# A new order of TensorE's steps in the attention stage of an attention and feed-forward kernel

## What is computed

```python
x = L0_attn_x                                   # 8192 rows of 512
xn = _layernorm(x)
x = x + infini_attention(xn, W_q, W_k, W_v, W_o, beta) + ffn(xn, ...)

def step(carry, qkv):                           # one segment of 64 rows, 16 heads of 32
    M, z = carry
    q, k, v = qkv
    sq = _sigma(q)                              # elu + 1
    denom_q = jnp.sum(sq * z[:, :, None, :], axis=-1, keepdims=True) + EPS
    A_mem = jnp.matmul(sq, M) / denom_q
    scores = jnp.where(causal, -jnp.inf, q @ k^T / sqrt(dk))
    A_dot = jnp.matmul(jax.nn.softmax(scores, axis=-1), v)
    A_s = beta * A_mem + (1.0 - beta) * A_dot
    sk = _sigma(k)
    denom_k = jnp.sum(sk * z[:, :, None, :], axis=-1, keepdims=True) + EPS
    V_prev = jnp.matmul(sk, M) / denom_k
    M_new = M + jnp.einsum('bhtk,bhtv->bhkv', sk, v - V_prev)
    z_new = z + jnp.sum(sk, axis=-2)
    return ((M_new, z_new), A_s)
# out = A_s of all segments @ W_o.T; 128 segments, one after the other
```

## Time and profile before

| | us |
|---|---|
| median of 3 runs | 1945.66 (1945.05 to 1948.57) |
| the profiled execution's own time | 1945.36 |
| its span, first to last instruction | 1943.6 |
| attention stage, from the span's start to about | 1260 |
| PE busy in the span | 1848.5 (95%) |
| mean granted clock of PE | 0.985 |

### The profile page before, as it was taken

The page is one execution under the profiler, slowest core; times in us unless marked ns, Lnnn a source line. Parts: engine busy times, 40 slices in busy tenths (PEclk is TensorE's granted clock), DMA queues, the critical chain, the costliest instruction groups (busy, mean ns, idle before and its releaser), DMA issues. The chain is left out here.

```text
span 1943.6 us, 72290 instructions
## 1 busy us (share of the span) xinstructions
PE 1848.5 (95%) x32348; PEld 1567.1 (81%) x32348; DVE 1445.2 (74%) x3477; ACT 875.7 (45%) x1494; POOL 148.7 (8%) x179
## 2 busy tenths in 40 slices
PE   6999999999999999999999999879899999879998
PEld 5888888888888888888888888657677777667997
DVE  6888788888887777787777777667588788876222
ACT  4443334343434443444434343325588787764110
POOL 2000000000000000000000000041100000001000
PEclk9999999999999999999999999879999999999999
DMA  4111211121121112111111110236500000015000
GB/s 147 47 46 58 73 52 46 58 74 52 46 74 52 36 36 61 43 36 40 59 41 36 47 51 30 95 95 183 164 26 12 13 12 23 13 41 161 17 12 22
DMA packets 65139, 108.45 MB, mean 56 GB/s; under 512 B 4720, under 2 KB 25216, under 8 KB 64832
## 3 DMA queue, kind: packets, MB, share of 16 engines
q1 hardware_dynamic: 59056, 84.69, 14.0%
q0 software_dynamic: 5776, 19.15, 3.2%
HBM read 59.26 MB, written 27.26 MB: 45 GB/s over the span
## 5 line engine op out<-in xcount | busy, mean ns | idle before, releaser
L1083 PE MATMUL proj<-xnT_high,held 128*128 128x256 f32 x1536 | 235.2, 288 | 3.3 <-DVE xnT_low L782 2.4
L1083 PEld LDWEIGHTS proj<-xnT_high,held 128*128 128x128 f32 x1536 | 203.6, 191 | 9.2 <-DVE xnT_low L782 2.9
L444 POOL TENSOR_TENSOR xs<-xs 128x512 f32<-128x512 f32 x63 | 80.9, 1285 | 1170.0 <-DVE xs L885 1170.0
L1083 PE MATMUL proj<-xnT_low,held 128*128 128x256 f32 x1024 | 163.7, 281 | 0.0
L2088 DVE CUSTOM_DVE_ANT_0 Sm<-Sp,held 128x1023 f32<-128x1023 f32 x128 | 155.5, 1216 | 8.0 <-DVE xs L2076 2.0
L1986 ACT ACTIVATE Sm<-Sm,least 128x1023 f32<-128x1023 f32 x128 | 146.7, 1146 | 14.1 <-DVE least L2088 13.3
L1083 PEld LDWEIGHTS proj<-xnT_low,held 128*128 128x128 f32 x1024 | 140.1, 190 | 0.0
L2141 PE MATMUL Sp<-KS,held 128*128 128x512 f32 x256 | 94.4, 451 | 29.9 <-DVE least L2088 25.6
L506 ACT ACTIVATE Pq<-Pq 128x1024 f32<-128x1024 f32 x63 | 66.9, 1062 | 123.4 <-DVE Pq L848 123.3
L486 ACT ACTIVATE QT<-proj 128x512 f32<-128x512 f32 x64 | 38.1, 595 | 182.4 <-PE proj L1083 182.4
L2038 DVE COPY PTs<-Tp 128x512 f32<-128x512 f32 x128 | 88.3, 690 | 29.7 <-PE Tp L2153 29.2
(11 more groups left out here) (343 smaller groups left out, 4341.2 us busy)
## 6 DMA issues: line engine op xcount, KB each, us to landing
VS<-DV SPq DMA_DIRECT2D x64, 264.0 KB, 3.9
xs<-in_x SPq DMA_DIRECT2D x32, 512.0 KB, 4.8
out_rows<-xs SPq DMA_DIRECT2D x64, 256.0 KB, 2.0
mask_columns<-x1T SPq DMA_DIRECT2D x16, 512.0 KB, 5.2
xs<-in_w SPq DMA_DIRECT2D x16, 512.0 KB, 3.8
xe<-in_x SPq DMA_DIRECT2D x15, 512.0 KB, 3.5
QT<-in_wqT SPq DMA_DIRECT2D x1, 1024.0 KB, 6.5
KT<-in_wkT SPq DMA_DIRECT2D x1, 1024.0 KB, 9.4
```

The lines of the kernel that those rows point to most:

```text
L444: pool.tensor_tensor(Ass[k], T1s[k], T2s[k], ALU.add).then_inc(s_as, 1)
L1083: ins = pe.matmul(bank[:, g * BT:g * BT + BT], w[hw][:, c, o:o + P], xnT[hx][:, c, :], start=n + c == 0, stop=n == 2 and c == G - 1)
```

## The change

PE, head of a half: AST1 goes in front of QT0; A/B 0 goes behind OUT1, directly in front of pv 0; T0 goes behind pv 0. PE, tail: behind memory 1 now come XT0, OUT0, XT1, T3, DEN, mask, scores, (in half 30 mask 1 and scores 1,) dent, SK1. The two banks get new lists. DVE: OUT0's add moves from the head of the next half into the tail of its own, denominators and reciprocals move from the tail into the next half, behind the row maximum and AST1's low part; softmax_part 0 comes ahead of m_next 0, m_next 3 behind the low part of XT1. ACT: AST1's high part ahead of the exponentials, the turned probabilities ahead of the negated A, XT1 ahead of DEN, SK1 last. `last` gets the denominators of the half before and loses OUT0's add. No instruction of work is added or removed.

```diff
--- before.py
+++ after.py
@@ -246,8 +246,8 @@
 
 
 
-        ORDER = (["AST1", "OUT1", "KT0", "KT1", "V1", "SK1", "DEN", "OUT0"],
-                 ["QT0", "QT1", "AST0", "V0", "SK0", "XT0", "XT1"])
+        ORDER = (["AST1", "OUT1", "KT0", "AST0", "V0", "SK0", "OUT0", "DEN"],
+                 ["QT0", "QT1", "KT1", "V1", "XT0", "XT1", "SK1"])
         FIRST = (["XF1", "QT1", "KT1", "V1", "SK1", "DEN"],
                  ["XF0", "QT0", "KT0", "V0", "SK0", "XT0", "XT1"])
 
@@ -534,13 +534,13 @@
             def half(m, p, first=False, ln=True):
                 pn = 1 - p
                 stage1 = True
-                prob(m, 0)
                 if not first:
                     a_t(m, 1)
+                prob(m, 0)
                 if stage1:
                     feature(m, 0, "QT", QT, pn, SCALE, (s_sk, m * 2 + 1))
+                p_turned(m, 0)
                 neg_a(m, 0)
-                p_turned(m, 0)
                 if stage1:
                     feature(m, 1, "QT", QT, pn, SCALE, (s_sk, m * 2 + 2))
                     feature(m, 0, "KT", KT, pn, 1.0, (s_sq, m * 2 + 3))
@@ -555,13 +555,12 @@
                     v_tile(m, pn, 1)
                 if stage1:
                     sk_tile(m, pn, 0)
-                    sk_tile(m, pn, 1)
                 if ln:
                     xT(m, "XT", 0)
+                    xT(m, "XT", 1)
                 if stage1:
                     den_rows(m)
-                if ln:
-                    xT(m, "XT", 1)
+                    sk_tile(m, pn, 1)
 
             high_w(0)
             xT(None, "XF", 0)
@@ -898,11 +897,12 @@
 
             def last(m, p):
                 pn = 1 - p
+                denominators(m - 1, m * 2, p)
+                reciprocals(p)
                 previous_values(m - 1, p)
                 row_max(m, 0, True)
                 less_max(m, 0)
                 m_next(m, 0)
-                out_rows(m - 1, m * 2 - 2, pn, 0)
                 row_max(m, 1, True)
                 less_max(m, 1, 1)
                 low_a(m, m * 2 - 1, 1)
@@ -930,10 +930,10 @@
                 row_max(m, 0)
                 less_max(m, 0)
                 if not first:
-                    out_rows(m - 1, m * 2 - 2, pn, 0)
+                    low_a(m, m * 2 - 1, 1)
+                    denominators(m - 1, m * 2, p)
+                    reciprocals(p)
                 previous_values(None if m == 0 else m - 1, p)
-                if not first:
-                    low_a(m, m * 2 - 1, 1)
                 if stage1:
                     sigma(m, "QT", 0, SQT[:, pn, 0:2, :], s_sq)
                 if look:
@@ -942,8 +942,8 @@
                     offer(m - CHOICE)
                 if not first:
                     out_rows(m, m * 2 - 1, pn, 1)
+                softmax_part(m, 0)
                 m_next(m, 0)
-                softmax_part(m, 0)
                 if first:
                     router(p, wcol[:, 0:2])
                 if m + 1 < AHEAD:
@@ -982,14 +982,12 @@
                 memory_part(m, p, 1)
                 if ln:
                     low_x(m, (m + 2) * 2, "XT", 0)
-                m_next(m, 3)
                 if look:
                     ahead_router(m, 1)
-                if stage1:
-                    denominators(m, n2, pn)
-                    reciprocals(pn)
+                out_rows(m, m * 2, p, 0)
                 if ln:
                     low_x(m, (m + 2) * 2, "XT", 1)
+                m_next(m, 3)
 
             def beta_factors():
                 dve.wait_ge(s_const, 1)
@@ -1277,16 +1275,16 @@
                 n = m + 1
                 n2 = (m + 1) * 2
 
+                if not first:
+                    as_transposes(m, m * 2 - 1, 1)
                 if stage1:
                     feature(m, "QT", wq, 0, ("XT", None if m == 0 else m - 1))
-                if not first:
-                    as_transposes(m, m * 2 - 1, 1)
-                a_and_b(m, p, 0)
                 p_transposes(m, 0)
                 if not first:
                     out_proj(m, 1)
+                a_and_b(m, p, 0)
+                pv(m, mh, p, 0)
                 t_times_m(m, 0)
-                pv(m, mh, p, 0)
                 if stage1:
                     feature(m, "QT", wq, 1)
                 memory(m, p, 0)
@@ -1309,22 +1307,21 @@
                 if stage1:
                     sk_rows(m, n2, 0)
                 memory(m, p, 1)
-                if stage1:
-                    sk_rows(m, n2, 1)
                 if ln:
                     x_transposes(m, m + 2, p, "XT", 0)
+                out_proj(m, 0)
+                if ln:
+                    x_transposes(m, m + 2, p, "XT", 1)
                 t_times_m(m, 3)
                 if stage1:
                     denominators(m, n, pn)
                     mask(m + 1, 0)
                     scores(pn, 0)
-                    den_transposes(m)
                     if m == NB - 2:
                         mask(m + 1, 1, True)
                         scores(pn, 1)
-                if ln:
-                    x_transposes(m, m + 2, p, "XT", 1)
-                out_proj(m, 0)
+                    den_transposes(m)
+                    sk_rows(m, n2, 1)
 
             pe.wait_ge(s_const, 1)
             x_transposes(None, 0, 0, "XF", 0)
```

## The result

The changed kernel took 1980.46 us in the median of 4 runs (1974.97 to 1984.92), the kernel before 1947.12 beside it; the ratio is 1.0167 (95% interval 1.0133 to 1.0201). Run once more later on, it gave 1981.28 us in the median of 5, ratio 1.0160 (1.0142 to 1.0179). So it is slower by 32 us. The direction was forecast, and the time lies 0.5 us inside the range of 1950 to 1981, 14 us above the forecast of 1966.0; the later median lies 0.3 us outside it, beside a kernel before that was slower too (1950.62). The profiled execution of after took 1974.97 us, its span is 1973.2, 29.6 more than before's.

A forecast was written before the change was run, and what follows sets the result against it. PE was taken to bound the attention stage, busy 1232 of 1260 us. Regular halves +15.6, instruction stops +4 and ends +1 made +20.6 on the span of 1943.6; forecast 1966.0 us, range 1950 to 1981.

The forecast's parts named there:

- The new wait at QT0: Head of each half: QT0 waits for SK1's bank copy, 1.43 us from start to start, a wait of 0.51.
- Head and tail: PE's steps per half: head 13.60 us, 2.38 less; tail 2.74 more plus 0.16 wait; together +0.52 a half.
- values and T0 step: Head of a half: values of tile 0 then T0 take 1.38 us together (1.33 to 1.45), saving a switch.
- DEN's wait in the look halves: Tail, first 15 halves, with router rows: DEN waits for OUT0's add, 0.16 us (0 to 0.3).
- Stops for instructions: PE stops at instruction-transfer edges: new ones in 9 of 30 halves, +10 us, old ones -5.7; net +4 (-6 to +12).
- None in the scores: The profile after would show "issue" stops in or behind T0 and no longer in the scores.
- Rival (c): Dense run starves PE: more or longer stops, slow clock behind some; +36 us, 1982; chance 0.13.
- The ends: Last two turns: OUT0 no longer separates denominators from A/B, weight copies come behind SK1's; about +1 us once (-1 to +3).
- (a): Rival: bank free in time for QT0, SK1's copy hidden behind AST1; 1935.2 us; chance 0.08.
- (b): Rival: small new wait and free DEN, +5.4 us, cancel against 5.7 of old stops that go; 1945 us; chance 0.10.
- (d): Rival: PE's clock falls in each half behind the new 0.5 us waits, 43 us more, 2008; chance 0.04.

The follow-up runs named there:

- experiment 4: The changed kernel with SK1 issued in front of the transposes of the denominators (dent) instead of behind them; 1972.75 us, ratio 1.0149.
- experiment 5: The changed kernel with OUT0's add ahead of the second router row on the vector engine in the 15 look halves; 1971.93 us, ratio 1.0150.
- experiment 1: The changed kernel with 120 additional semaphore increments at the start of PE's program; 1973.77 us, ratio 1.0154.
- experiment 9: The kernel before with one repeated 64x33 value product in 16 halves, 14 repeats in half 26 and 38 semaphore increments at the start; 1953.62 us, ratio 1.0027.
- experiment 2: The changed kernel with 168 additional semaphore increments at the start of PE's program; 1997.36 us, ratio 1.0273.

## Why the prediction was right in direction and short in size

**The new wait at QT0: right.** SK1 to QT0 was put at 1.43 (1.30 to 1.55) from rows 4, and measured at 1.38 in every regular half; experiment 4 shows that it is the bank's turn. 0.46 a half over 30 halves makes 13.8 of the 15.3 us forecast. That one turn in the trace of before was worth more than any reasoning on the copy's length.

**Head and tail: right to 0.02 us in the later halves.** Head 13.60 forecast and 13.60 measured (13.49 in halves with a QT0 of 2.80), tail 6.86 forecast and 6.85 measured. In the values and T0 step I took 1.38 of 1.33 to 1.45; it is 1.45. This and the 0.05 at QT0 cancel.

**DEN's wait in the look halves: wrong, 0.16 (0 to 0.3) forecast, 0.52 measured (0.10 in the later halves).** The step put the router row ahead of OUT0's add at "about 0.7 us". Alone it takes 0.69; beside POOL's add it took 1.46. It need not have been a surprise: in the trace of before the same row, at 348.55, takes 1.12, with POOL's add from 347.85 to 349.12:

```profile
347.85 1.27 POOL L444 TENSOR_TENSOR xs<-xs 128x512 f32<-128x512 f32 x1 [17.23 <-DVE xs L885]
...
348.55 1.12 DVE L648 CUSTOM_DVE_ANT_0 ln<-xe,xs 128x512 f32<-128x512 f32 x1
```

In both traces the row ends 0.55 us behind POOL's add, and so, to 0.01, in all 15 look halves of each: 0.69 of its own work begun 0.14 before POOL's end. In experiment 5, where it meets no add, it takes 0.68. By that sum OUT0's add could have been placed. The Trainium skill (SBUF — State Buffer, "🔬 SBUF: two separate sides") has the rule: a vector instruction with two SBUF inputs and a GpSimd instruction that reads SBUF lock the same port pair, and the later one is blocked for the whole of the other. The row reads two SBUF tensors, and the traces agree but for the 0.14. The term was worth 14 x 0.42 = 5.9 us. With the later halves at 0.46 in place of 0.52, the regular halves together came to 14 x 0.86 + 16 x 0.46 = 19.4 us against the 15.6 forecast.

**Stops for instructions: place and kind right, sum short.** Forecast: in or behind T0, 1.3 us each, in 9 of 30 halves, none left in the scores. Measured in the first trace: 7 halves, 0.6 to 1.65 us each, 9.4 in all, 1.5 for a slow clock behind one, and about 2 in small stops at A/B, SK1 and AST1 that I did not have; less the 5.7 that go, +7 against +4 (the spans of halves 1 to 29 leave 6.2 beside the regular halves). The range of -6 to +12 holds it. The +4 itself was summed too low: 9 halves at 1.3 us are 11.7 and not 10. "None in the scores" holds for the first trace; the second has one of 1.5 us there in half 30, and experiment 1 one of 1.2. Rival (c) had 9 stops of 2.2 us and a slow clock of 1.4 us behind 4 of them; in T0 and QT1 there was one such slow clock in each of the two traces. The time came out near this rival's 1982, but by DEN's wait and the ends as much as by stops.

**The ends: +1 (-1 to +3) forecast, +2.9 measured, and half 30 +1.2** (start -0.6, half 0 +0.7, the last turn and all behind it +2.8; half 30 is +1.7, of which 0.46 is the regular half). Half 30 has its own DEN behind OUT0, where T3 to DEN is 0.95, and a KT1 of 3.38. In half 0 the trace of before has a stretch at 1.2 GHz of 6.8 us, the first trace of after none, and the second has one again. The +2.8 is made of two larger terms that I had not seen. The last turn and the start of the feed-forward part are 4.4 us shorter than before's; some 2.9 of it will be before's stop of 1.1 us and slow clock, as experiment 9, which keeps before's order and has no such stop, is 2.9 us ahead at the same place. And one stretch of the feed-forward part, from the 2000th to the 800th product before the end, is 7.2 us longer, though no instruction of it was changed. In order before, after, and experiment 5:

```profile
1662.88:1809.71 146.83, 128.22 (x1208) 103.94 (x1201) 102.64 (x184) 79.02 (x130) 7.88 (x8) 0.99 0.23 73
1685.26:1839.33 154.07, 133.38 (x1209) 108.92 (x1202) 102.74 (x184) 79.12 (x130) 7.66 (x8) 0.94 0.22 69
1686.89:1833.74 146.85, 128.19 (x1208) 103.93 (x1201) 102.68 (x184) 78.88 (x130) 7.89 (x8) 0.99 0.23 73
```

The granted clock is 0.94 in the long one and 0.99 in the short ones, and the second trace of after shows the same (154.2 us at 0.94). Places of edges can't be the cause: all three kernels have the same count of instructions, and experiment 5 takes the 146.85 of before. This stretch alone is more than the 5.6 us by which the span of experiment 5 lies below after's. What makes the clock fall there in one kernel and not in the other stays open. That the time still lies in the range, by 0.5 us, is in part luck: 7.2 us more and 4.4 less, neither of them in the sum, half cancel.

**The rivals.** (a) and (b) needed a free or cheap bank and are out. (d), a clock that falls in each half behind the waits of 0.5 us, did not come: the granted clock of the regular halves is 1.00, with a wait in each. What the Trainium skill tells of another kernel (TensorE: Matmul & The Clock Gate, "A second HAM failure mode: psum-queue depth-cycling") finds no support in the stage here. In halves 1 to 30 of the two traces the clock fell only behind stops of 1.2 us and more, and not behind all of them; half 0 and the part behind the stage have slow stretches of their own.

**What made the median 5.5 us worse than the profiled run** can't be read from a trace of that group, as the slower executions have none. The trace of the later one points the same way: it has the same waits for banks (9.9 and 8.1 us) and the stage 6.7 longer by stops and slow clock. A forecast by one profiled execution can't have that, and my 0.30 us between the profiled run and the median was taken over from a kernel with few stops. Taken together, for the 29.6 us of the profiled execution: about 14 are QT0's turn and 6 DEN's wait in look halves (19.4 with the small terms that go the other way), 6 the stops of halves 1 to 29 with their clock, 1.2 half 30, and 2.9 the ends, in which -4.4 and +7.2 stand against each other. The first two are shown by experiments 4 and 5, the places of the stops by 1 and 2, and the +7.2 has no cause shown.

## What to carry to other kernels

When a move brings short steps together on two banks, look in the trace for a turn of the same kind (product, copy, next product: 1.38 to 1.43 us here) and count what work lies inside it; in-turn work is free, and an order that looks equal in sum is not. When a step comes behind another on the vector engine, take its price beside what POOL will do at that moment, not its price alone. And count PE's instructions along a change that packs small products: here an edge in the last part of 320 instructions in 2.2 us, or just behind it, cost 0.6 to 1.9 us each time. But do not tune the count for one stage, as every later stage moves with it, and compare the untouched stages of two traces before a difference of the whole is given to the change.

## What the runs showed of the hardware

- PE's stops for instructions in halves 0 to 30 stand at 192 (to within 3) past a multiple of 256 of its own count: 168 instructions added at the start moved all seven one half ahead, as named beforehand. Nearly all of the long ones had a dense run in front (288 instructions in 2.2 to 2.8 us in T0 and QT1). The rule of the dense run does not explain all: stops of 0.3 to 1.0 us stood at AST1 and SK1 with 288 instructions in 6.8 to 7.2 us in front (halves 17, 20 and 23 of the changed kernel), one of 1.4 in the scores with 6.4 (experiment 2, half 27), and one of 0.9 in the large products of OUT0 with 4.6 (experiment 9, half 24).
- Semaphore increments are dear: 48 more of them moved the first dent by 6.4 us, 0.13 us each. Repeating a 64x33 product into the same place cost 0.10 us, where one of the 32 in the value product costs 1.07/32 = 0.03.
- A vector instruction of 0.69 us with two inputs in SBUF took 1.04 to 1.13 us beside a POOL add before the change and 1.45 to 1.46 after it, in all 30 cases to 0.54 or 0.55 us behind that add's end.
- The same 1200 products of the feed-forward part took 146.8 to 154.2 us in the twelve traces, and the granted clock of the stretch was highest (0.99) in the two shortest and lowest (0.94) in the two longest.
- The same program has the same stops each time, but not of the same length: waits of 1.05 and 1.00 us in half 10, T0 of 1.93 and 2.12 in half 13 and of 1.79 and 2.17 in half 28, in two executions, with the clock falling behind other ones. Whether this sets the spread of the times isn't shown: the changed kernel's runs spread over 10 us the first time and 3.5 the second, and experiment 4, with the same stops, over 2.5.
